# 1444-key attention: the full-array job of a key tile moves from in front of the tile's weighing to behind it

## The chip, the cores and the metric

The kernel runs on one core of a Trainium2 chip. The metric is the device time of one execution in microseconds (us), the median over several runs. Clocks and durations inside an execution come from one profiled execution.

## What is computed

Two decoder layers over 32 sequences of 100 tokens with 128 features. The part that matters here is the second layer's cross attention: 16 heads of 8 features attend from 100 tokens to 1444 context keys, for each of the 32 sequences.

```python
qm = split_heads(q @ Wq.T + bq);  km = split_heads(k @ Wk.T + bk);  vm = split_heads(v @ Wv.T + bv)
scores = einsum('bnlh,bnph->bnlp', qm, km) / sqrt(8)
scores = where(mask, scores, -1e8)
attn = softmax(scores, axis=-1)
out = einsum('bnlp,bnph->bnlh', attn, vm)      # then out @ Wo.T + bo
```

The softmax takes a maximum over the keys for each head and token, so scores are worked out twice: once for the maxima, once for the weights.

## The kernel before

The program has a setup and three stages. Stage A (self attention, first cross attention, gated feed-forward) and stage C (the last feed-forward with its experts) are not touched. Stage B (`stage_b`) is the attention above. It goes over 8 groups of 4 sequences: `n` is the sequence, `g` its group, `j` its place in the group.

For a sequence the keys are cut in 12 key tiles (`kt` 0 to 11) of 128 keys. TensorE's program, `slots`, goes through the key tiles and does three kinds of work in each:

- Scores. Four pieces (`score_piece`, p 0 to 3) work out the scores of the next key tile from 64 rows of the array each (L1304): pieces 0 and 1 on one half of the rows, 2 and 3 on the other. ScalarE takes the exponent of the results of two pieces at a time into `PT` (`exponent`, L1198).
- Ring jobs. Everything else that TensorE has to do for this or the next two sequences is cut into jobs (`job`), which write one PSUM bank each, of three banks in turn (`RING = (4, 5, 7)`). A job waits until the job three places ahead of it in the ring has been drained. Most jobs are maxima (L1285): one 64-row matmul with 482 keys, placed ahead of a score piece that uses the other half of the rows. VectorE drains each with a reduction (L1408).
- Weighing. `weigh` (L1320) multiplies `PT` of the tile with the values: 8 matmuls (16 instructions) in four column strips of 32, which all end in bank 6.

The rest of the ring jobs use all 128 rows; these are the full-array jobs. They stand at place `PHASES * kt + 4`, one place behind the last score piece of the tile:

| kt | maxima, on which pieces | full-array jobs | drained by |
|---|---|---|---|
| 0 | 4, on pieces 0 1 2 3 | queries of the next group: three for j = 0, one for j = 1 and 2, none for j = 3 | VectorE |
| 1 | 3, on 0 1 2 | the divisor of the sequence before ("result", L1267) | VectorE, one reciprocal (L1402) |
| 2 | 3, on 0 2 3 | value (L1272) | ScalarE copy (L1181) |
| 3 | 3, on 0 1 2 | value | ScalarE copy |
| 4 | 3, on 0 2 3 | value, the last of three | ScalarE, two copies |
| 5 | 3, on 0 1 2 | one query for j = 0 and 1 (L1256); leftover maximum (L1282) | VectorE |
| 6 | 3, on 0 2 3 | leftover maximum; key (L1261) | VectorE |
| 7 | 2, on 0 2 | leftover maximum; key | VectorE |
| 8 | none | turn of the maxima (L1289); key | VectorE (key: L1398) |
| 9, 10, 11 | 4, on 0 1 2 3 | none | |

A query job that is a "stack" (L1256) has three VectorE instructions behind it (L1382, L1385, L1386), of which the first frees the bank. VectorE drains strictly in ring order. The order of work is written out by hand (`MAIN_TILES`, `QUERY_SLOTS`, `ring_jobs`) and is fixed. The last sequences have fewer jobs: the last group has no queries, sequence 30 has no keys to prepare, and sequence 31 has only its result job.

`exponent` waits, ahead of its first half, for `pv_done` of the weighing two tiles back; `weigh` waits for the exponents of its own tile, for which the third score piece of the same tile has waited already.

Of the kernel before, what the change touches and what calls it, by code (L numbers as in the profile page):

```python
# [909 lines left out]
def ring_jobs(g, j, last):  # L910

    nxt = not last or j + 1 < GROUP
    after = not last or j + 2 < GROUP
    jobs = [((g, j + 1, "result", 0), PHASES * 1 + 4)]
    for i, (_, _, _, kt, p) in enumerate(MAINS):
        if i < EARLY and after:
            jobs.append(((g, j + 2, "max", i), PHASES * kt + p))
        if i >= EARLY and nxt:
            jobs.append(((g, j + 1, "max", i), PHASES * kt + p))
    if not last:  # L920
        jobs += [((g + 1, 0, "query", r), PHASES * kt + 4) for r, kt in QUERY_SLOTS[j]]
    if nxt:
        jobs += [((g, j + 1, "value", r), PHASES * (r + 2) + 4) for r in range(3)]
        jobs += [((g, j + 1, "max", len(MAINS) + c), PHASES * (c + 5) + 4) for c in range(3)]
        jobs.append(((g, j + 1, "turn", 0), PHASES * 8 + 4))
    if after:
        jobs += [((g, j + 2, "key", r), PHASES * (r + 6) + 4) for r in range(3)]
    return sorted(jobs, key=lambda job: job[1])
# [14 lines left out]
def stage_b(nc, t, ctxt, mask, pen_dram, h3t, att):  # L943
# [6 lines left out]
    with ExitStack() as ctx:  # L950
# [29 lines left out]
        def wait(engine, semaphore, value):  # L980

            if not (isinstance(value, int) and value <= 0):
                engine.wait_ge(semaphore, value)
# [16 lines left out]
        def place(g, j, i):  # L1000

            first = g if isinstance(g, int) else 1
            return starts[first, j] + i, (0 if isinstance(g, int) else g - 1)
# [230 lines left out]
        def _(pe):  # L1234
# [57 lines left out]
            def score_piece(g, j, kt, p):  # L1292

                n = g * GROUP + j
                half, a = divmod(p, 2)
                if kt == 0 and p == 0:
                    pe.wait_ge(t.ks_loaded[j % 2], (2 * g + (j // 2 + 1)) * 16 * KS_DMAS)
                    pe.wait_ge(t.qrow_loaded[j % 2], (2 * g + (j // 2 + 1)) * 64)
                    pe.wait_ge(sem["qexp_ready"], n + 1)
                if a == 0:  # L1300
                    wait(pe, sem["pt_ready"], n * 2 * KT + (2 * kt + half - 1))
                rows = slice(ROW * half, ROW * half + ROW)
                for s in (2 * a, 2 * a + 1):
                    m = mm(bank(p, D, 2 * T, (s % 2) * 2 * T), KS[rows, j % 2, s, kt * D:(kt + 1) * D],  # L1304
                           QS[rows, j % 2, s * 2 * T:(s + 1) * 2 * T], start=True, stop=True)
                if a:
                    m.then_inc(sem["st_psum"], 1)

            def weigh(g, j, kt):

                n = g * GROUP + j
                pe.wait_ge(sem["pt_ready"], n * 2 * KT + (2 * kt + 2))
                if kt == 0:
                    wait(pe, sem["att_free"], n)
                    pe.wait_ge(sem["v_drained"], 3 * (n + 1))


                for b in range(2):
                    for r in range(4):
                        m = mm(psum[32 * r:32 * r + 32, 6, b * 2 * T:(b + 1) * 2 * T], V[:, j % 2, kt, 4 * b + r, :],  # L1320
                               PT[:, kt % 2, 2 * b + r // 2, (r % 2) * 2 * T:(r % 2 + 1) * 2 * T],
                               start=(kt == 0 and b == 0), stop=(kt == KT - 1), tile_position=(0, 32 * r),
                               skip_group_check=True)
                m.then_inc(sem["pv_done"], 1)

            def slots(g, first, last):
                for j in range(GROUP):
                    jobs = ring_jobs(g, j, last)

                    def some(k):  # L1330
                        for i, (what, where) in enumerate(jobs):
                            if where == k:
                                job(*place(g, j, i), *what)

                    for kt in range(KT):

                        ahead = (j, kt + 1) if kt + 1 < KT else (j + 1, 0)
                        for p in range(4):
                            some(PHASES * kt + p)
                            if not last or ahead[0] < GROUP:  # L1340
                                score_piece(g, *ahead, p)
                        some(PHASES * kt + 4)
                        weigh(g, j, kt)

            for i, what in enumerate(first_ring_jobs()):
                job(i, 0, *what)
# [1 line left out]
            for p in range(4):  # L1348
                score_piece(0, 0, 0, p)
            slots(0, True, False)  # L1350
            for g in range(1, GROUPS - 1):
                slots(g, False, False)
            slots(GROUPS - 1, False, True)

            job(END, 0, GROUPS - 1, GROUP + 1, "result", 0)
# [888 lines left out]
```

## Time and profile before

| | |
|---|---|
| runs | 2407.42, 2407.45, 2408.70 us; median 2407.45 |
| profiled execution, its own time | 2401.97 us |
| its span, first to last instruction | 2400.2 us |
| maxima in stage B, first to last (L1285) | 643.0 to 1784.5 us |
| whole execution: PE, DVE, ACT, POOL busy | 85%, 66%, 55%, 22% |
| granted clock of TensorE, mean | 0.917 |

PE is TensorE's matmuls and PEld its weight loads, DVE is VectorE, ACT ScalarE, POOL GpSimd. The profiled execution is 0.23% below the median of the runs. A row of the timeline gives start, length, engine, line, operation, tiles, shapes and count; in brackets stands how long the engine was idle ahead of it and what ended that. Matmuls overlap, so PE can be shown as busy although it does not run at its full rate, and a row's length ends when its last result is out.

### The profile page before, as it was taken

The numbers are of one execution on the slowest core, as the hardware profiler recorded it, in microseconds if no ns is written. First come the engines' busy times: TensorE is split into PE (matmuls) and PEld (weight loads), VectorE is DVE, ScalarE is ACT, GpSimd is POOL, SyncE is SP. The second block draws the span as 40 slices with busy tenths as digits, with TensorE's granted clock in tenths as the row PEclk, the third lists the DMA queues.
The fourth block names the chain that finished last, engine by engine and source line by source line (L and its number), as shares of the span: only waits on it lengthen the run. The fifth ranks groups of instructions, "written<-read, shape, count | busy, mean of one in ns | idle before, by whom it ended". The sixth has DMA issues, their size and how long they took to land. (4 is left out here: it accounts for less than half of the span.)

```text
span 2400.2 us, 45166 instructions
## 1 busy us (share of the span) xinstructions
PE 2028.5 (85%) x17914; PEld 1347.5 (56%) x17914; DVE 1583.8 (66%) x3854; ACT 1320.0 (55%) x2169; POOL 535.9 (22%) x476
## 2 busy tenths in 40 slices
PE   3779997466599999999999999999996888878997
PEld 2546665343355556556565555556564565656776
DVE  5844543787578878877877878878862566654443
ACT  3645554576246666666666666666673555543333
POOL 1410000553302212212222212212212233221111
PEclk9789997666589999999999999999997898879999
DMA  5026662000222313313323323313312110000000
GB/s 160 1 86 187 186 186 75 4 18 17 90 69 104 115 64 113 114 64 117 107 77 108 107 72 113 115 62 115 115 43 94 35 36 18 1 1 4 8 8 11
DMA packets 89104, 181.18 MB, mean 75 GB/s; under 512 B 5907, under 2 KB 63163, under 8 KB 88511
## 3 DMA queue, kind: packets, MB, share of 16 engines
q1 hardware_dynamic: 88894, 178.30, 22.6%
q8 instruction: 143, 2.34, 0.4%
q14 instruction: 67, 0.54, 0.1%
HBM read 95.24 MB, written 11.65 MB: 45 GB/s over the span
## 5 line engine op out<-in xcount | busy, mean ns | idle before, releaser
L1408 DVE TENSOR_REDUCE b_part_max<-psum 128x1 f32<-128x482 f32 (+3 forms) x1248 | 737.3, 650 | 187.6 <-PE psum L1285 173.6
L1198 ACT ACTIVATE b_PT<-psum 128x800 f32<-128x800 f32 x768 | 616.4, 836 | 386.0 <-PE psum L1304 380.0
L1285 PE MATMUL psum<-b_KH,b_QBD 64*128 64x482 f32 (+1 forms) x1152 | 421.4, 443 | 46.3 <-DVE b_part_max L1408 43.4
L1304 PE MATMUL psum<-b_QS,b_KS 64*128 64x200 f32 x3072 | 438.7, 288 | 0.5 <-ACT b_PT L1198 0.3
L1304 PEld LDWEIGHTS psum<-b_QS,b_KS 64*128 64x128 f32 x3072 | 339.6, 186 | 16.2 <-issue 12.1
L1320 PE MATMUL psum<-b_PT,b_V 128*32 128x200 f32 x6144 | 341.1, 339 | 0.6 <-ACT b_PT L1198 0.6
L1285 PEld LDWEIGHTS psum<-b_KH,b_QBD 64*128 64x128 f32 x1152 | 196.6, 188 | 198.0 <-DVE b_part_max L1408 118.6
L1121 POOL TENSOR_TENSOR b_KL<-b_KF,b_KH 128x1444 fp32r<-128x1444 f32 x32 | 106.8, 3337 | 691.9 <-PE psum L1304 669.7
L1320 PEld LDWEIGHTS psum<-b_PT,b_V 128*32 128x32 f32 x6144 | 159.9, 109 | 149.0 <-ACT b_PT L1198 82.3
L2096 DVE SCALAR_TENSOR_TENSOR c_U<-psum,c_gt,c_U 100x128 f32<-100x128 f32 x256 | 72.1, 344 | 129.0 <-PE psum L1917 128.8
L384 POOL TENSOR_TENSOR a_rs<-a_ve,a_half 100x4 f32<-100x4 f32 x48 | 50.0, 1041 | 420.7 <-DVE a_ve L757 420.6
L1917 PE MATMUL psum<-c_W,c_HE 128*100 128x128 f32 x1024 | 123.6, 274 | 14.1 <-ACT c_HE L1682 14.0
L1917 PEld LDWEIGHTS psum<-c_W,c_HE 128*100 128x100 f32 x1024 | 117.2, 167 | 31.8 <-ACT c_HE L1682 18.7
L1272 PE MATMUL psum<-W,b_CT 128*128 128x128 f32 (+1 forms) x768 | 117.7, 293 | 12.7 <-DVE b_part_max L1408 6.7
L804 DVE TENSOR_REDUCE a_peak<-psum 100x1 f32<-100x1446 f32 x32 | 53.2, 1664 | 105.3 <-PE psum L629 105.3
L1272 PEld LDWEIGHTS psum<-W,b_CT 128*128 128x128 f32 (+1 forms) x768 | 92.7, 188 | 41.4 <-DVE b_part_max L1408 37.4
L1682 ACT ACTIVATE c_HE<-psum,C 128x400 f32<-128x400 f32 x128 | 71.9, 587 | 78.9 <-PE psum L1906 75.9
L1646 ACT COPY c_PT<-psum 100x800 f32<-100x800 f32 x64 | 52.5, 821 | 102.0 <-PE psum L1810 102.0
L636 PE MATMUL psum<-a_P,a_CN 128*128 128x100 f32 (+1 forms) x768 | 108.0, 288 | 0.0
L1261 PE MATMUL psum<-b_CT,W 128*128 128x482 f32 (+1 forms) x192 | 101.2, 611 | 5.5 <-DVE b_QF L1382 1.5
L636 PEld LDWEIGHTS psum<-a_P,a_CN 128*128 128x128 f32 (+1 forms) x768 | 95.2, 195 | 18.7 <-issue 11.8
L1535 POOL TENSOR_TENSOR c_rs<-c_ve,c_half 100x4 f32<-100x4 f32 x24 | 24.4, 1015 | 337.0 <-DVE c_ve L1998 337.0
(274 smaller groups left out, 3204.3 us busy)
## 6 DMA issues: line engine op xcount, KB each, us to landing
b_KS<-b_KH SPq DMA_DIRECT2D x64, 722.0 KB
a_CT<-in_ctxt SPq DMA_DIRECT2D x32, 722.0 KB, 4.2
b_CT<-in_ctxt SPq DMA_DIRECT2D x32, 722.0 KB, 4.3
b_KS<-b_KL SPq DMA_DIRECT2D x32, 722.0 KB
a_CN<-in_ctxn SPq DMA_DIRECT2D x32, 704.0 KB
att_scratch<-b_AO SPq DMA_DIRECT2D x32, 200.0 KB, 1.9
c_AIN<-att_scratch SPq DMA_DIRECT2D x8, 800.0 KB
b_MB<-in_mask SPq DMA_DIRECT2D x32, 180.5 KB, 4.4
```

The lines of the kernel that those rows point to most:

```text
L636: x_ = mm(bank(7, D, T, TG), CN[0:rows, m % 3, k, :], PTA[0:rows, m % 2, k, :], start=(k == 0), stop=(k == KT - 1))
L1121: pl.tensor_tensor(KL[:, :], KF[:, 0:S], KH[:, j % 2, :].bitcast(F32), ALU.subtract).then_inc(sem["kl_ready"], 1)
L1198: nc.scalar.activation(PT[:, kt % 2, 2 * a:2 * a + 2, :], psum[:, 2 * a:2 * a + 2, 0:TG], ACT.Exp).then_inc(sem["pt_ready"], 1)
L1261: m = mm(bank(b, D, size), w("xkT"), CT[:, j % 2, c:c + size], start=True, stop=True)
L1272: m = mm(bank(b, rows, D, (k % 4) * D), CT[:, j % 2, k * D:k * D + rows], w("xvT"), start=True, stop=True)
L1285: m = mm(bank(b, D, size), QBD[rows, j % 2, tile * D:(tile + 1) * D], KH[rows, j % 2, at_:at_ + size], start=True, stop=True)
L1304: m = mm(bank(p, D, 2 * T, (s % 2) * 2 * T), KS[rows, j % 2, s, kt * D:(kt + 1) * D], QS[rows, j % 2, s * 2 * T:(s + 1) * 2 * T], start=Tr ...
L1320: m = mm(psum[32 * r:32 * r + 32, 6, b * 2 * T:(b + 1) * 2 * T], V[:, j % 2, kt, 4 * b + r, :], PT[:, kt % 2, 2 * b + r // 2, (r % 2) * 2 ...
L1408: v.tensor_reduce(part_max[0:rows, q, c:c + 1], bank(b, rows, CHUNKS[c][1]), AX.X, ALU.max)\
L1682: nc.scalar.activation(HE[:, n % 2, f, :], bank((2 * n + f) % 4, D, TG), ACT.Relu, bias=t.C[:, c:c + 1]).then_inc(sem["moe_h_ready"], 1)
L1917: x_ = mm(bank(4 + n % 2, T, D, j * D), HE[:, n % 2, f, t.ts_(j)], W2[:, c * D:(c + 1) * D], start=(f == 0), stop=(f == 1))
L2096: last = v.scalar_tensor_tensor(out=U3[:, u % 2, j, :], in0=tok_bank(4 + n % 2)[:, j, :], scalar=gt[:, u, 6, j * EXPERTS + e:j * EXPERTS + ...
```

## The change

In each key tile the weighing is issued straight behind the last score piece, and the full-array jobs of the tile behind the weighing. No instruction is added or removed.

```diff
@@ -1339,8 +1339,8 @@
                             some(PHASES * kt + p)
                             if not last or ahead[0] < GROUP:
                                 score_piece(g, *ahead, p)
+                        weigh(g, j, kt)
                         some(PHASES * kt + 4)
-                        weigh(g, j, kt)
```

`some(k)` issues the ring jobs whose place is `k`. The other engines' programs are unchanged.

## Rows read from the trace of the kernel before

**Rows 1.** Windows, stage B at its steady rate: busy time, count, clock, DMA share, GB/s.
```profile
700.00:1760.00 1060.00, 984.03 (x10766) 622.86 (x10765) 852.27 (x1520) 678.30 (x946) 244.82 (x174) 1.00 0.28 96
```

**Rows 2.** The page's groups of instructions: the drain of maxima, weight load of values.
```profile
L1408 DVE TENSOR_REDUCE b_part_max<-psum 128x1 f32<-128x482 f32 (+3 forms) x1248 | 737.3, 650 | 187.6 <-PE psum L1285 173.6
...
L1272 PEld LDWEIGHTS psum<-W,b_CT 128*128 128x128 f32 (+1 forms) x768 | 92.7, 188 | 41.4 <-DVE b_part_max L1408 37.4
```

**Rows 3.** Timeline of PE, sequence 15, key tiles 1 and 2.
```profile
1231.20 0.48 PE L1285 MATMUL psum<-b_KH,b_QBD 64*128 64x482 f32 x1
...
1231.74 0.62 PE L1304 MATMUL psum<-b_QS,b_KS 64*128 64x200 f32 x4
1232.43 0.94 PE L1267 MATMUL psum<-b_OD,K 128*128 128x200 f32 x4
1233.30 0.89 PE L1320 MATMUL psum<-b_PT,b_V 128*32 128x200 f32 x16
1234.13 0.48 PE L1285 MATMUL psum<-b_KH,b_QBD 64*128 64x482 f32 x1
...
1234.90 0.46 PE L1285 MATMUL psum<-b_KH,b_QBD 64*128 64x482 f32 x1
...
1235.57 1.16 PE L1272 MATMUL psum<-W,b_CT 128*128 128x128 f32 x8 [0.22 <-DVE b_part_max L1408]
1236.66 0.89 PE L1320 MATMUL psum<-b_PT,b_V 128*32 128x200 f32 x16
```

**Rows 4.** Timeline of DVE in the same stretch.
```profile
1233.43 1.40 DVE L1402 RECIPROCAL b_RD<-psum 128x200 f32<-128x200 f32 x1
```

**Rows 5.** Timeline of ACT in the same stretch.
```profile
1236.77 0.59 ACT L1181 COPY b_V<-psum 128x512 f32<-128x512 f32 x1 [0.34 <-PE psum L1272]
```

**Rows 6.** Timeline of PE, the same sequence, weighings of key tiles 3 to 6.
```profile
1239.80 0.89 PE L1320 MATMUL psum<-b_PT,b_V 128*32 128x200 f32 x16
...
1243.05 0.89 PE L1320 MATMUL psum<-b_PT,b_V 128*32 128x200 f32 x16
...
1245.11 0.44 PE L1282 MATMUL psum<-b_KH,b_QBL 128*64 128x482 f32 x1
1245.48 0.88 PE L1320 MATMUL psum<-b_PT,b_V 128*32 128x200 f32 x16
...
1248.09 1.08 PE L1261 MATMUL psum<-b_CT,W 128*128 128x482 f32 x2
1249.09 0.89 PE L1320 MATMUL psum<-b_PT,b_V 128*32 128x200 f32 x16
```

**Rows 7.** Timeline of PE, sequence 13, key tiles 5 and 6, with a query.
```profile
1173.78 0.94 PE L1256 MATMUL psum<-b_HT,W 128*128 128x400 f32 x2
...
1174.87 0.88 PE L1320 MATMUL psum<-b_PT,b_V 128*32 128x200 f32 x16
...
1177.21 0.48 PE L1285 MATMUL psum<-b_KH,b_QBD 64*128 64x480 f32 x1 [0.59 <-DVE b_part_max L1408]
...
1179.35 0.89 PE L1320 MATMUL psum<-b_PT,b_V 128*32 128x200 f32 x16
```

**Rows 8.** Timeline of DVE in that stretch.
```profile
1174.78 0.62 DVE L1382 TENSOR_SCALAR b_QF<-psum,xbq 128x400 f32<-128x400 f32 x1
...
1176.51 2.91 DVE L1408 TENSOR_REDUCE b_part_max<-psum 64x1 f32<-64x482 f32 x5
```

**Rows 9.** Timeline of PE, sequence 15, key tile 9: first and fourth maximum.
```profile
1255.43 0.48 PE L1285 MATMUL psum<-b_KH,b_QBD 64*128 64x482 f32 x1
...
1256.67 0.48 PE L1285 MATMUL psum<-b_KH,b_QBD 64*128 64x482 f32 x1 [0.30 <-DVE b_part_max L1408]
```

**Rows 10.** Timeline of DVE there: the drain of the key job.
```profile
1254.72 0.72 DVE L1398 SCALAR_TENSOR_TENSOR b_KF<-psum,C,b_MB 128x480 f32<-128x480 f32 x1
```

**Rows 11.** Timeline of PE, sequence 16, key tile 0: fourth maximum, three queries.
```profile
1264.06 0.48 PE L1285 MATMUL psum<-b_KH,b_QBD 64*128 64x482 f32 x1 [0.29 <-DVE b_part_max L1408]
...
1264.63 1.62 PE L1253 MATMUL psum<-b_HT,W 128*128 128x136 f32 x6
```

## The prediction

> **What bounds the kernel now.** I read the page first, then stage B in windows, then who waits for whom on PE, then the timelines of PE, DVE and ACT over single key tiles. The window over the steady part of stage B shows PE busy for 984.03 of 1060.00 us at the full granted clock of 1.00 (2.4 GHz), DVE for 852.27 and ACT for 678.30 [rows 1]. So stage B goes at the pace of PE's instruction stream, and DVE, at 80%, is close behind. What PE does wait for is the ring: in each group of idle time the releaser is DVE's reduction of a maximum. The reader is to see in the timelines that the stage is regular to 0.02 us: the same key tile of another sequence with the same jobs takes the same time. So one sequence of each kind can be walked through and multiplied by its count.
>
> **What the change does.** It removes and adds nothing. It moves the full-array jobs of a key tile one weighing later. The weighing takes 0.82 us of PE (1233.30 to 1234.13, and 1174.87 to the next tile's start; I use 0.82) [rows 3, 7]. No DMA is issued by what is moved, and SP's and POOL's queues keep their order; their inputs (the turned maxima, the reciprocal) come up to 0.82 us later relative to the tile, and PE never waits for them now. Behind the moved jobs on PE now stand the next tile's scores and maxima directly.
>
> Two things follow, of opposite sign. First, a full-array job waits for the drain of the job three ahead of it, now just before it starts: the value job at 1235.57 shows 0.22 us idle for that [rows 3]. Behind a weighing this wait is over. Second, the job's own drain is what the third ring job behind it waits for, in the next tile a maximum. Before, that drain had the weighing and two pieces as cover; after, the pieces alone.
>
> **Prices that I use.** Changing between scores, weighing and full array, the next kind starts 0.06 to 0.07 us ahead of the modelled end of the last: result 1232.43+0.94=1233.37, weighing at 1233.30; weighing 1233.30+0.89=1234.19, maximum at 1234.13 [rows 3]. Slots, start to start: result 0.87, value 1.09 (1235.57 to 1236.66) [rows 3], leftover maximum 0.37, key 1.00 [rows 6], query stack with leftover maximum 1.09 (1173.78 to 1174.87) [rows 7]. The third value job needs 1.20: key tile 4 takes 3.25 (weighing to weighing, 1239.80 to 1243.05), less 1.23 for scores and wait and 0.82 [rows 6]. A bank is free for PE 0.05+0.65+0.06 us after the modelled end of a maximum (drain 650 ns [rows 2]; the fourth maximum at 1256.67 waits for the first, of 1255.43: 0.48+0.05+0.65+0.06=1.24) [rows 9]. Drains behind one another follow every 0.57 (five in 2.91) [rows 8]. From the last maximum to the next kind it is 0.41 where one piece follows (0.48−0.07) [rows 9] and 0.55 where two follow (0.62−0.07 from 1231.74) [rows 3]. So with maxima on 0 1 2 the third starts at 0.54 and scores end at 1.09; on 0 2 3 it starts at 0.77 and they end at 1.18 [rows 3].
>
> The one turn that no row shows is weighing to full array. I take it at 0.07 of overlap like the other three. The bounds: 0.05 us worse on each, or a first weight load of 0.19 us (188 ns [rows 2]) wholly under the weighing, so 0.12 to 0.19 better. The Trainium skill bears on this. "TensorE: Matmul & The Clock Gate", Part 2, step 1, says that TensorE pulls weight loads ahead of running matmuls where row groups don't collide or the background buffer takes them; that would give the better end. "TensorEngine Tiling", Key Properties, says that a change of tiling mode drains the engine; by that rule the trace agrees, since no turn above gains more than 0.07 us.
>
> **Tile by tile**, from the start of a tile's scores to that of the next, after minus before:
>
> - kt 0, three queries (7 sequences). The fourth maximum starts at 1.23. Before, the queries start 0.57 behind it (1264.06 to 1264.63) [rows 11]; scores alone end at 0.41, so 0.16 is wait. Between the three a further wait of about 0.24 shows (1.55 for their slots against 3×0.44, six matmuls with a step of some 0.22, an estimate from this row). After: −0.40, bounds −0.16 to −0.40; ×7 = −2.8.
> - kt 0, one query (14): −0.16; ×14 = −2.2.
> - kt 1, no single query ahead (18): 2.93 before (1231.20 to 1234.13) [rows 3]; after 1.09+0.82+0.87 = 2.78. −0.15; ×18 = −2.7. With one query ahead (14) its chain of three DVE instructions takes 1.73 (1174.78 to 1176.51) [rows 8] and now delays the third maximum by 0.27 and, through the first maximum's drain, the result job; this comes to 0.
> - kt 2 (31), the largest. Count from the start of kt 1's scores. Weighing at 1.09, result job at 1.91, its end at 2.85, reciprocal 0.06 later for 1.40 [rows 4]: 2.91 to 4.31, seen by PE at 4.37. The scores of kt 2 start at 2.78; their third maximum wants 3.55 and gets 4.37: 0.82 idle. Scores end at 4.78, weighing, value at 5.60 without a wait, next scores at 6.69. That is 3.91 against 3.36 (1233.30 to 1236.66) [rows 3]: +0.55; ×31 = +17.1.
> - kt 3 (31). The value job started at f=5.60; ends at f+1.16, copy at f+1.20 for 0.59 [rows 5], seen at f+1.85; scores started at f+1.09, so their third maximum goes at 0.76, not 0.54. 0.76+0.55+0.82+1.09 = 3.22 against 3.14 (1236.66 to 1239.80) [rows 3, 6]: +0.08; ×31 = +2.5.
> - kt 4 (31). Third maximum wants 0.77, no stall: 1.18+0.82+1.20 = 3.20 against 3.25 [rows 6]: −0.05; ×31 = −1.6.
> - kt 5 (31). As kt 3, third maximum at 0.76: 1.31+0.82+0.37 = 2.50 against 2.43 (1243.05 to 1245.48) [rows 6]; about +0.08 with a query as well; ×31 = +2.5.
> - kt 6, no query ahead (16). The leftover maximum's drain lets the third maximum go at 0.83: 1.24+0.82+0.37+1.00 = 3.43 against 3.61 (1245.48 to 1249.09), whose waits between scores, leftover and key go [rows 6]: −0.18; ×16 = −2.9.
> - kt 6, query ahead (14). Query at f, end f+0.94, DVE chain from f+1.00 for 1.73, leftover drain to f+3.38, seen at f+3.44 [rows 7, 8]. Scores start at f+1.09, so the third maximum goes at 2.35, where it went at 1.52 (1177.21 against 1175.69, which is 1174.87+0.82) [rows 7]. 2.35+0.41+0.82+0.37+1.00 = 4.95 against 4.48 (1174.87 to 1179.35) [rows 7]: +0.47; ×14 = +6.6.
> - kt 7, 8: 0, no third maximum and no wait of note.
> - kt 9 (30). The key job of kt 8 ends 0.07 behind the start of the scores; drain 0.12 to 0.84 [rows 10]; the third maximum goes at 0.90 (wanted 0.54). The first maximum's drain is queued behind it: 0.84 to 1.49, so the fourth goes at 1.55 where it went at 1.24 [rows 9]: +0.31; ×30 = +9.3. DVE has caught up by kt 10; 10 and 11: 0.
>
> Sum: +17.1+2.5+2.5+6.6+9.3 = +38.0 and −2.8−2.2−2.7−1.6−2.9 = −12.2: **+25.8 us**, all of it in stage B. The profiled execution would go from 2401.97 to 2427.8; on the median 2407.45, 0.23% above it, I predict **2433**. The same walk with the order of before gives the before rows to 0.02 us a tile, with nothing fitted but the slots. A change within 0.2%, or 5 us, is what a measurement of this kernel can't tell from none.
>
> **Rivals.**
>
> - A, cover only: the third maxima don't stall, as the banks come free in time. Then each tile keeps the gains: kt 0 and 1 −7.7; kt 2 (1.18+0.82+1.09=3.09) −0.27×31; kt 3 (3.00) −0.14×31; kt 4 −1.6; kt 5 (2.28) −0.15×31; kt 6 −0.23×16 and −0.35×14: −35, so 2372. Against it: the maximum at 1177.21 does stall, 0.59 of it shown, for just such a drain, with the weighing as cover still [rows 7]. Chance 0.04.
> - B, on the faster side: weighing to full array costs less than the other turns, with the first weight load under the weighing. 32 sequences have 8 such turns and three in four a ninth, some 270. At 0.19 each −51 against +26: 2382. It decides from 0.10 a turn (26/270). Against it: the three other turns hold at 0.06 to 0.07 [rows 3]. Chance 0.04; another 0.04 for a part of it that ends within 5 us of before. (The page on the clock gate, Part 2 of the Trainium skill, is the one that speaks for B.)
> - C, no change, 2407: DVE's and PE's waits only change places. That needs kt 2's reciprocal and kt 9's key drain off the ring's path, and both are on it by the ring rule. In the 0.04 above.
> - D, slower still: the stall in kt 6 behind a query, 1.58 long, brings PE's clock down to 1.2 GHz, where rows 1 show 1.00 throughout. If kt 7 then ran at half rate, some 2.5 us more for each of 14: 2468. Chance 0.04.
>
> **How the numbers follow.** Forecast 0.84. Its own range: ±0.05 on 270 turns is ±13, and the query estimate 2 more: 2419 to 2447. That range leaves out A, B and D, 0.12 in all, and a margin of the forecast's own; it is the range I give. Faster 0.08, same 0.04, slower 0.88.
>
> **What the profile after would show.** Third maximum of kt 2 idle for about 0.8 us behind the reciprocal, value and result jobs without idle ahead of them; period of kt 2 3.91, of kt 6 behind a query 4.95, of kt 9 2.78; a group of four sequences 3.3 us longer than now; clock 1.00 in stage B; stage A and C unchanged. Full-array jobs starting more than 0.07 before the end of a weighing would show B. What would make me wrong above all is that turn, and the reciprocal's drain overlapping otherwise than in the walk.

## The result and the profile after

The changed kernel takes 2428.34 us (median of 7 runs, 2425.01 to 2430.20) against 2407.45 (7 runs): ratio 1.0083, 95% interval 1.0069 to 1.0097. Slower, as forecast; 2433 was predicted, in a range of 2419 to 2447. The profiled execution took 2428.34 us with a span of 2426.6.

Stage B holds most of the difference. Its scores (L1304) run from 682.9 to 1814.1 us before and from 685.9 to 1836.0 after: 1131.2 against 1150.1, +18.9. The other 7.5 us between the two spans lie ahead of and behind the scores, where no code is changed. Over the ten profiled executions of this document the part ahead of the first score takes between 682.3 and 696.8 us and the part behind the last between 582.2 and 594.2, in no order that follows the edits, so this part of the difference is scatter.

The stage B window of the changed kernel; columns as in [rows 1]:

```profile
700.00:1780.00 1080.00, 1001.93 (x10796) 646.31 (x10796) 857.83 (x1521) 683.55 (x947) 245.14 (x174) 0.99 0.27 94
```

The clock is 0.99, not 1.00. What PE waited for in that window, longest in total first (us in total, times, longest):

```profile
PE psum L1285 <- DVE b_part_max L1408: 42.6, 101, 1.3
PE psum L1285 <- DVE b_RD L1402: 18.5, 29, 0.6
PE psum L1285 <- DVE b_KF L1398: 5.4, 30, 0.2
PE psum L1267 <- DVE b_part_max L1408: 3.6, 14, 0.3
```

Two new waits stand there, both of maxima (L1285): one for the reciprocal, once in each sequence, and one for the key's drain. The wait of the value job, which the same view of the kernel before (700 to 1760 us) shows, is gone from the list:

```profile
PE psum L1272 <- DVE b_part_max L1408: 6.3, 29, 0.2
```

Now the stretch of [rows 3], sequence 15, key tiles 1 and 2, after the change, on PE:

```profile
1245.44 0.48 PE L1285 MATMUL psum<-b_KH,b_QBD 64*128 64x482 f32 x1
...
1246.54 0.89 PE L1320 MATMUL psum<-b_PT,b_V 128*32 128x200 f32 x16
1247.36 0.94 PE L1267 MATMUL psum<-b_OD,K 128*128 128x200 f32 x4
1248.23 0.48 PE L1285 MATMUL psum<-b_KH,b_QBD 64*128 64x482 f32 x1
...
1249.80 0.48 PE L1285 MATMUL psum<-b_KH,b_QBD 64*128 64x482 f32 x1 [0.64 <-DVE b_RD L1402]
...
1250.21 0.88 PE L1320 MATMUL psum<-b_PT,b_V 128*32 128x200 f32 x16
1251.02 1.16 PE L1272 MATMUL psum<-W,b_CT 128*128 128x128 f32 x8
1252.11 0.48 PE L1285 MATMUL psum<-b_KH,b_QBD 64*128 64x482 f32 x1
```

and on DVE, the answer to [rows 4]:

```profile
1248.34 1.41 DVE L1402 RECIPROCAL b_RD<-psum 128x200 f32<-128x200 f32 x1 [0.58 <-PE psum L1267]
```

The reader is to see four things. The weighing ends, as modelled, at 1246.54+0.89=1247.43, and the result job starts at 1247.36: the turn that no row had shown overlaps by 0.07 us like the others. The third maximum of key tile 2 starts 1.57 us into the tile (1249.80 against 1248.23), 0.8 later than it could; the prediction's walk through the tile had 1.59. The value job starts with no idle ahead of it. And the tile takes 1252.11−1248.23=3.88, where 3.91 was forecast and 3.36 measured before.

The profile gives each tile of each sequence. Measured change of the tiles' lengths, summed over sequences 0 to 30, beside the prediction's terms:

| key tile | before, us | after, us | sum measured | sum forecast |
|---|---|---|---|---|
| 0, three queries / one | 4.18 / 3.49 | 3.42 / 3.33 | −6.9 | −5.0 |
| 1 | 2.93 (3.45 behind one query) | 2.79 to 2.84 (3.44) | −2.1 | −2.7 |
| 2 | 3.36 | 3.89 | +16.4 | +17.1 |
| 3 | 3.14 | 3.28 | +4.2 | +2.5 |
| 4 | 3.25 | 3.18 | −2.4 | −1.6 |
| 5, with query / without | 3.13 / 2.41 | 3.32 / 2.60 | +5.7 | +2.5 |
| 6, behind query / not | 4.48 / 3.62 | 4.74 at full clock / 3.21 | +2.8, with the half clock told below | +3.7 |
| 7 | 3.06 | 2.85 | −5.3 | 0 |
| 9 | 2.47 | 2.68 | +6.4 | +9.3 |
| 8, 10, 11 | 2.47 | 2.47 | 0 | 0 |
| all | | | +18.8 | +25.8 |

Two rows fall out of the walk. Key tile 7 became shorter, and in four sequences (0, 8, 12 and 20, all with j = 0) key tiles 6 and 7 together take 1.57 us more than elsewhere. For the second, sequence 12 (PE, the stretch that answers to [rows 7]):

```profile
1149.76 0.48 PE L1285 MATMUL psum<-b_KH,b_QBD 64*128 64x480 f32 x1
...
1152.10 0.48 PE L1285 MATMUL psum<-b_KH,b_QBD 64*128 64x480 f32 x1 [1.28 <-DVE b_part_max L1408]
...
1152.51 1.56 PE L1320 MATMUL psum<-b_PT,b_V 128*32 128x200 f32 x16
1154.00 0.66 PE L1282 MATMUL psum<-b_KH,b_QBL 128*64 128x482 f32 x1
1154.46 1.69 PE L1261 MATMUL psum<-b_CT,W 128*128 128x482 f32 x2
1156.08 0.49 PE L1285 MATMUL psum<-b_KH,b_QBD 64*128 64x480 f32 x1
```

The third maximum goes 2.34 us into the tile, as forecast (2.35): 1.57 later than the 0.77 at which it could, and 1.28 of that is shown as idle. Behind it everything is slow: the weighing takes 1.56 us and not 0.89. Three windows of PE alone (busy time and count, then the granted clock), and the stall and what follows it in sequence 13, where the same stall has no such sequel:

```profile
1149.00:1152.00 3.00, 1.82 (x11) 1.00 0.00 0
1152.60:1155.60 3.00, 3.00 (x19) 0.50 0.00 0
1156.20:1159.20 3.00, 3.00 (x33) 1.00 0.02 5
1189.00:1191.60 2.60, 1.50 (x10) 1.00 0.00 0
1191.80:1195.00 3.20, 3.20 (x32) 1.00 0.00 0
```

TensorE is at 0.50, that is 1.2 GHz, right behind the stall in sequence 12, and at 1.00 in sequence 13. This is rival D, which had a chance of 0.04 and put 2.5 us on each of 14 places. It came in 4 of them, in this one execution, at 1.57 us each, 6.3 us in all.

For key tile 7, weight loads (PEld) of its leftover maximum and key job. After, sequence 12:

```profile
1157.76 0.13 PEld L1282 LDWEIGHTS psum<-b_KH,b_QBL 128*64 128x64 f32 x1 [0.32 <-DVE b_part_max L1408]
1157.81 0.41 PEld L1261 LDWEIGHTS psum<-b_CT,W 128*128 128x128 f32 x2
1158.93 0.42 PEld L1304 LDWEIGHTS psum<-b_QS,b_KS 64*128 64x128 f32 x6 [0.71 <-ACT b_PT L1198]
```

Before, sequence 15:

```profile
1250.76 0.13 PEld L1282 LDWEIGHTS psum<-b_KH,b_QBL 128*64 128x64 f32 x1
1251.13 0.30 PEld L1261 LDWEIGHTS psum<-b_CT,W 128*128 128x128 f32 x2 [0.24 <-DVE b_part_max L1408]
1252.14 0.33 PEld L1320 LDWEIGHTS psum<-b_PT,b_V 128*32 128x32 f32 x12 [0.71 <-ACT b_PT L1198]
```

Before, the key's first weight load waits for a bank and starts 0.37 us behind that of the leftover maximum. After, the bank is free by then and the load starts 0.05 us behind it, under the running matmul. The matmuls of the same two jobs, after and before:

```profile
1157.76 0.43 PE L1282 MATMUL psum<-b_KH,b_QBL 128*64 128x480 f32 x1
1158.03 0.97 PE L1261 MATMUL psum<-b_CT,W 128*128 128x482 f32 x2
...
1250.76 0.44 PE L1282 MATMUL psum<-b_KH,b_QBL 128*64 128x480 f32 x1
1251.13 1.08 PE L1261 MATMUL psum<-b_CT,W 128*128 128x482 f32 x2
```

Leftover and key take 1158.93−1157.76=1.17 us together and not 1252.14−1250.76=1.38. Half of the gain is an earlier start of the key (0.27 us behind the leftover and not 0.37), half a shorter key (0.90 to the next kind and not 1.01).

### The profile page after: what moved, and what is told of

Its sections match the earlier page's. It is cut to its first block and busy times, and to the rows that moved or that the text cites. A ratio compares the mean times of both kernels' runs of the same rounds, so it can differ in the third digit from the quotient of the medians.

```text
span 2426.6 us, 45166 instructions
## 1 busy us (share of the span) xinstructions
PE 2055.2 (85%) x17914; PEld 1376.2 (57%) x17914; DVE 1591.2 (66%) x3854; ACT 1324.3 (55%) x2169; POOL 536.6 (22%) x476
## 3 DMA queue, kind: packets, MB, share of 16 engines
q8 instruction: 143, 2.34, 0.4%
## 5 line engine op out<-in xcount | busy, mean ns | idle before, releaser
L1285 PE MATMUL psum<-b_KH,b_QBD 64*128 64x482 f32 (+1 forms) x1152 | 460.8, 457 | 80.2 <-DVE b_part_max L1408 44.0
L1304 PE MATMUL psum<-b_QS,b_KS 64*128 64x200 f32 x3072 | 483.9, 294 | 0.6 <-ACT b_PT L1198 0.3
L1304 PEld LDWEIGHTS psum<-b_QS,b_KS 64*128 64x128 f32 x3072 | 360.0, 187 | 27.8 <-ACT b_PT L1198 25.4
L1285 PEld LDWEIGHTS psum<-b_KH,b_QBD 64*128 64x128 f32 x1152 | 200.3, 188 | 272.4 <-DVE b_part_max L1408 152.6
L1906 PE MATMUL psum<-c_YT,c_W 128*128 128x400 f32 x256 | 98.1, 506 | 0.0
```

Source lines behind the costliest of these rows:

```text
L1285: m = mm(bank(b, D, size), QBD[rows, j % 2, tile * D:(tile + 1) * D], KH[rows, j % 2, at_:at_ + size], start=True, stop=True)
L1906: mm(bank((2 * n + f) % 4, D, TG), W1[:, c * D:(c + 1) * D], YT[:, u, :], start=True, stop=True).then_inc(sem["moe_h_psum"], 1)
```

## The experiments

Ratios are against the kernel before, whose median beside these kernels was 2410.02 for the first four and 2410.07 for the last four. Two theories stood against each other. One is late drains: the prediction's walk, with the slots of key and queries corrected by the profile above. The other is an even cost of the turn from weighing to full array, which the total of 20 us on 270 turns does not exclude.

Times of whole executions scatter by some us, mostly outside stage B, so for each kernel the length of stage B in its profiled execution is given too, from its first score to its last (L1304):

| kernel | stage B, us | against before | against changed |
|---|---|---|---|
| before | 1131.2 | | |
| changed | 1150.1 | +18.9 | |
| result job alone behind | 1144.4 | +13.2 | |
| result job alone in front | 1138.2 | | −11.9 |
| query tile in front | 1132.5 | | −17.6 |
| key tiles 6 and 7 alone | 1108.5 | −22.7 | |
| copy, order of before | 1124.8 | −6.4 | |
| copy, changed order | 1122.1 | | −28.0 |
| long chain | 1177.0 | | +26.9 |
| only the jobs that gain | 1098.7 | −32.5 | |

### One job moved: the result job alone behind the weighing

```diff
-                        weigh(g, j, kt)
-                        some(PHASES * kt + 4)
+                        if kt != 1:
+                            some(PHASES * kt + 4)
+                            weigh(g, j, kt)
+                        else:
+                            weigh(g, j, kt)
+                            some(PHASES * kt + 4)
```

> The order of before, with the result job of key tile 1 alone behind its weighing. Theory (late drains: what costs is that the job's drain now comes too late for the third ring job behind it): key tile 1 falls from 2.93 to 2.78 us (3.50-less case 3.44 to 2.78 behind a query), key tile 2 rises from 3.36 to about 4.19, as its third maximum stalls 0.8 behind the reciprocal and the value job then waits too; about +14 us, 2421. Rival (the cost is spread evenly: each of some 270 turns from weighing to full array costs about 0.075 us, which makes the 20 us of the change): 31 turns, +2 us, 2410, and key tile 2 stays at 3.36.

Measured: 2427.34 us, ratio 1.0068 (1.0044 to 1.0093), +16. Sequence 15 on PE, its key tile 2:

```profile
1247.50 0.49 PE L1285 MATMUL psum<-b_KH,b_QBD 64*128 64x482 f32 x1
...
1249.07 0.48 PE L1285 MATMUL psum<-b_KH,b_QBD 64*128 64x482 f32 x1 [0.64 <-DVE b_RD L1406]
...
1249.77 1.16 PE L1272 MATMUL psum<-W,b_CT 128*128 128x128 f32 x8 [0.21 <-DVE b_part_max L1412]
1250.86 0.89 PE L1320 MATMUL psum<-b_PT,b_V 128*32 128x200 f32 x16
1251.68 0.48 PE L1285 MATMUL psum<-b_KH,b_QBD 64*128 64x482 f32 x1
```

Key tile 2 takes 1251.68−1247.50=4.18 us (forecast 4.19); key tile 1 fell to 2.75 to 2.79. The third maximum stalls behind the reciprocal, and as the value job is still in front it waits too. An even cost of a turn would give +2 us. This one moved job of some nine costs by itself 13.2 us of stage B, where the whole change costs 18.9.

### The mirror: the result job alone in front

The condition is `kt == 1` for the order of before, all else as changed.

> The changed order, with the result job of key tile 1 alone back in front of its weighing. Late drains: key tile 2 falls from 3.89 to 3.09 us (no stall behind the reciprocal, and no wait ahead of the value job), key tile 1 is 2.93, but 4.26 behind a single query (its result waits in front for a drain queue that the query has delayed); together -12 us against the changed kernel, about 2416. Even cost of a turn: -2 us, 2426.

Measured: 2414.07 us, ratio 1.0024 (1.0010 to 1.0039). Key tile 2 takes 3.08, key tile 1 2.93 and, behind one query, 4.26. So taking the same job out of the changed kernel gives most of the loss back. Four half-clock stretches are there again, two of them in key tile 6 behind the query and two in key tile 1 behind one query, where the result job now waits 1.1 us. One of the latter, sequence 17:

```profile
1318.12 1.25 PE L1267 MATMUL psum<-b_OD,K 128*128 128x200 f32 x4 [1.07 <-DVE b_part_max L1412]
1319.29 1.56 PE L1320 MATMUL psum<-b_PT,b_V 128*32 128x200 f32 x16
```

### The query tile in front

The condition is `kt == 5 and j < 2`.

> The changed order, with the jobs of key tile 5 back in front of the weighing for the two sequences of a group that have a query there. Late drains: key tile 6 behind the query falls from 4.74 to 3.93 us, its third maximum stalling 0.75 and not 1.57; -12 us, and, if the four stretches of half clock seen in the changed kernel come from the long stall, these go too and give some 5 us more: about 2411. Even cost of a turn: 14 turns fewer, -1 us, 2427; and half clock would be seen as before.

Measured: 2410.14 us, ratio 1.0001 (0.9987 to 1.0015). The stretch of [rows 7] on PE:

```profile
1179.39 0.48 PE L1285 MATMUL psum<-b_KH,b_QBD 64*128 64x480 f32 x1
...
1180.91 0.48 PE L1285 MATMUL psum<-b_KH,b_QBD 64*128 64x480 f32 x1 [0.59 <-DVE b_part_max L1412]
...
1183.30 0.48 PE L1285 MATMUL psum<-b_KH,b_QBD 64*128 64x480 f32 x1
```

The third maximum goes at 1.52 as before the change, key tile 6 takes 3.91 (forecast 3.93), and the clock is 1.00 from 700 to 1760 us. The other jobs stay moved, and the kernel is level with the kernel before. Of the 17.6 us of stage B that this gives back, 14 times 0.82 are the tile and 6.3 the half clock.

### The key tiles 6 and 7 alone

The condition is `kt not in (6, 7)`.

> The order of before, with the jobs of key tiles 6 and 7 (leftover maximum and key) alone behind the weighing. Late drains: nothing queued behind them is late enough to stall, and the gains stand alone. Their waits go, and the key's weight load, no longer held by a wait, slides under the leftover maximum: key tile 6 falls from 4.48 to 3.93 us behind a query and from 3.62 to 3.17 without, key tile 7 from 3.05 to 2.86; about -22 us against before, 2386. Even cost of a turn: 60 turns, +4 us, 2412.

Measured: 2385.59 us, ratio 0.9911 (0.9893 to 0.9929). Key tile 6 takes 3.93 behind a query and 3.07 else (forecast 3.17), key tile 7 2.85. Sequence 15, its key tile 7 on PE, without a wait:

```profile
1238.54 0.48 PE L1285 MATMUL psum<-b_KH,b_QBD 64*128 64x480 f32 x1
...
1240.21 0.43 PE L1282 MATMUL psum<-b_KH,b_QBL 128*64 128x480 f32 x1
1240.48 0.97 PE L1261 MATMUL psum<-b_CT,W 128*128 128x482 f32 x2
1241.38 0.70 PE L1304 MATMUL psum<-b_QS,b_KS 64*128 64x200 f32 x8
```

So two of the moved places are worth 23 us of stage B by themselves, and the same edit that makes the kernel slower as a whole makes it faster there.

### The reciprocal made short, in either order

```diff
-                    v.reciprocal(RD[:, :], bank(b, D, PAIRED // 2)).then_inc(drained, 1)
+                    v.tensor_copy(RD[:, :], bank(b, D, PAIRED // 2)).then_inc(drained, 1)
```

The copy leaves out the reciprocal, so the output is not the attention's; the kernels serve to time the order alone. In the order of before:

> The order of before, with the reciprocal of the divisor (1.40 us on VectorE) replaced by a copy of the same 128x200 elements, so that the output is not the attention's; a copy should take some 0.4 us. Late drains: the drain is hidden in this order but for the value job's wait; key tile 2 falls from 3.36 to 3.15 us, -7 us against before, 2403. If the reciprocal played no part in key tile 2: nothing.

and in the changed order:

> The changed order with the same copy in place of the reciprocal. Late drains: the third maximum of key tile 2 no longer stalls, and key tile 2 falls from 3.89 to 3.09 us: -25 us against the changed kernel, 2403, level with the same copy in the order of before (-5 us by the walk, the half-clock stretches taking that back). Even cost of a turn: the copy changes both orders alike, and this one stays 20 us above the other, 2423.

Measured: 2403.27 us, ratio 0.9973 (0.9957 to 0.9990), and 2398.56 us, ratio 0.9954 (0.9939 to 0.9969). The changed order with the copy, on DVE and then on PE:

```profile
1229.72 0.37 DVE L1402 COPY b_RD<-psum 128x200 f32<-128x200 f32 x1 [0.58 <-PE psum L1267]
```

```profile
1229.61 0.48 PE L1285 MATMUL psum<-b_KH,b_QBD 64*128 64x482 f32 x1
1229.62 0.88 PE L1304 MATMUL psum<-b_QS,b_KS 64*128 64x200 f32 x7
...
1230.39 0.37 PE L1285 MATMUL psum<-b_KH,b_QBD 64*128 64x482 f32 x1
...
1232.60 0.48 PE L1285 MATMUL psum<-b_KH,b_QBD 64*128 64x482 f32 x1
```

With a drain of 0.37 us and not 1.41 the third maximum goes at 0.78, without a stall, and key tile 2 takes 2.99. In the order of before it takes 3.14. The order of before gets 7 us from the shorter drain and the changed order some 30 (28 in stage B, where 25 were expected, the tile being 0.1 shorter than expected), and the changed order is then no longer the slower one. Four half-clock stretches stand behind the 14 long stalls of key tile 6 here too. What the change costs in key tile 2 hangs on the length of this one drain.

### The long chain made longer

In the changed order the third instruction of a query stack is issued twice:

```diff
+                    link(v.scalar_tensor_tensor(out=QR[:, g % 2, s, :], in0=QH[:, :].bitcast(F32), scalar=K[:, K_NEG1:K_NEG1 + 1],
+                                                in1=QF[:, :], op0=ALU.mult, op1=ALU.add))
                     m = v.scalar_tensor_tensor(out=QR[:, g % 2, s, :], in0=QH[:, :].bitcast(F32), scalar=K[:, K_NEG1:K_NEG1 + 1],
                                                in1=QF[:, :], op0=ALU.mult, op1=ALU.add)
```

> The changed order, with the third VectorE instruction of each query stack issued twice in a row, 0.64 us longer (the result is the same). Late drains: key tile 6 behind a query rises from 4.74 to 5.40 us, its stall from 1.57 to 2.2, and key tile 1 behind one query from 3.44 to 4.10; 28 times 0.66 is +18 us against the changed kernel, 2447. If the long stall is what brings half clock, there are more than the four stretches of the changed kernel, up to one behind each of the 14 stalls, and 2450 to 2465; if these stretches have another cause, about four again.

Measured: 2456.87 us, ratio 1.0196 (1.0178 to 1.0215), 0.0113 or 27 us above the changed kernel's 1.0083; 28 times 0.66 and five half-clock stretches more at 1.57 make 26, and stage B grew by 26.9. Key tile 1 behind one query takes 4.11 (forecast 4.10); key tile 6 behind the query takes 5.42 at full clock and 6.96 where half clock follows. Sequence 13 on PE:

```profile
1213.21 0.48 PE L1285 MATMUL psum<-b_KH,b_QBD 64*128 64x480 f32 x1
...
1216.22 0.70 PE L1285 MATMUL psum<-b_KH,b_QBD 64*128 64x480 f32 x1 [1.95 <-DVE b_part_max L1410]
...
1216.85 1.56 PE L1320 MATMUL psum<-b_PT,b_V 128*32 128x200 f32 x16
```

Half clock now follows in 9 of 14 such tiles, and seven of the nine are those at j = 1, one in every group. So the stalls of one execution are no independent draws, and each count here is that of one execution. A stall of 1.28 us of shown idle was followed by half clock in 4, 4 and 2 of 14 places (the changed kernel, the changed order with the copy, the result job in front), one of 1.95 in 9 of 14, and in the six kernels whose longest idle in stage B's steady part is 0.65 us there is none. Taking the stall away took the half clock away, and making it longer brought more. So the stall brings it. Why one stall of the same length is followed by it and the next is not, none of these runs shows.

### Only the jobs that gain

The order of before, with the jobs of key tiles 3, 6 and 7 behind the weighing, and those of key tile 0 for j = 0 (`if not (kt in (3, 6, 7) or kt == 0 and j == 0)` keeps the old order).

> Behind the weighing stand only the jobs that the walk says gain there: those of key tiles 3, 6 and 7, and of key tile 0 for the sequence with three queries. Late drains: key tile 0 with three queries 3.42 us, key tile 3 3.00, key tile 6 3.93 behind a query and 3.07 without, key tile 7 2.85, the rest as before, no half clock; -31 us against before, 2379. Even cost of a turn: some 100 turns, +7 us.

Measured: 2380.73 us, ratio 0.9876 (0.9857 to 0.9895), −30. Key tile 0 with three queries takes 3.42, key tile 3 2.97, key tile 6 3.93 and 3.07, key tile 7 2.85, the others as before. It beats both kernels. Stage B is 32.5 us shorter than before, where 31 was expected. In the window at its steady rate the clock is 1.00:

```profile
700.00:1730.00 1030.00, 967.96 (x10801) 631.22 (x10800) 855.76 (x1520) 678.99 (x946) 244.79 (x174) 1.00 0.29 99
```

PE issues 10801 matmuls in 1030 us, where 10766 took 1060 [rows 1].

## Why the prediction was right

- What bounds the kernel: right. Stage B goes at PE's stream, and the idle time in it belongs to the ring. With the slots corrected by the profile after, the tile lengths named in the expectations of eight further kernels came out within 0.10 us, most within 0.03.
- First effect, the wait in front of a full-array job goes: right. The value job starts without a wait, and where the gains stand alone they are worth 23 us of stage B (key tiles 6 and 7) and 33 (all the jobs that gain).
- Second effect, the job's drain loses the weighing as cover: right, and the larger of the two in the changed kernel. It was shown from both sides, by moving the result job alone and by taking it back alone, and by shortening the drain.
- The turn from weighing to full array: 0.07 us of overlap, as taken (1247.43 against 1247.36), so rival B is out. For comparison, the key job behind the leftover maximum, with both on all 128 rows, starts 0.16 us ahead of the end (1157.76+0.43=1158.19 against 1158.03). The Trainium skill, "TensorEngine Tiling (Array Packing)", Key Properties, has a change of tiling mode drain the engine; the trace agrees in so far as this turn overlaps less than that one.
- Key tiles 6 and 7: mis-sized. The terms of key tile 6 and "kt 7, 8: 0" took 1.00 us for a key job, from a row in which it had waited for its bank. For key tile 7 "no wait of note" was wrong too: the key's weight load waits 0.24 us there. Without the wait leftover and key take 1.17 and not 1.37: 0.20 in each of some 60 tiles, 12 us, nearly all that the sum was too high. The Trainium skill, "TensorE: Matmul & The Clock Gate", Part 2, step 1, has weight loads pulled ahead of running matmuls. The trace agrees here: as soon as no wait holds it, the key's load starts 0.05 us behind the leftover's, while the leftover maximum runs.
- Smaller terms: three queries in a row gain 0.76, where the bounds were 0.16 to 0.40, as behind the weighing they take 0.95 us together and not 3×0.44; a stalled third maximum with two pieces behind it needs 0.62 to the end of the scores and not 0.55 (key tiles 3 and 5: +9.9 and not +5.0); in key tile 9 the first maximum's drain starts 0.63 behind the key's and not 0.72 (+6.4 and not +9.3). They cancel to about 1 us.
- Half clock, put at 0.04 as rival D with 35 us, came in part: four stretches, 6.3 us. Summed: 25.8−13.3+6.3=18.8 us in stage B. The walk was 13.3 us too high, and the half clock made up 6.3 of it. Of the 7 us that were left in stage B the medians show 5 (20.9 between them, 25.6 forecast), and the 2 us between are scatter outside it. Without the half clock the change would have been some 12.5 us in stage B, which on the median of before is 2420, at the lower end of the range. That part of the closeness is luck.

## What to carry to other kernels

In a ring of buffers a job has two times that matter: the wait in front of it, and the moment by which its drain must be over for the job one ring length behind. Moving it later helps the first and hurts the second, so it has to be priced for each job by the length of its drain, and the answer can differ in sign between neighbours: here two places of one edit gained 23 us of stage B and a third lost 13. A slot that was read from a row with a wait in it is too long for an order in which the wait is gone, and a stall that is made longer may cost more than its own length through the clock.

## What the runs showed of the hardware

A stall of PE shown as 1.28 us idle, between stretches at full clock, was followed by half clock in 4, 4 and 2 of 14 places in three kernels, one of 1.07 us in 2 of 14, and one of 1.95 us in 9 of 14; each time it cost 1.4 to 1.6 us beside the wait. Waits of 0.65 us had none behind them, nor had the 14 of 0.9 us in key tile 1 of the long chain. A weight load that waits for a bank loses its place under the matmul ahead of it: the pair of leftover maximum and key took 1.38 us with a wait of 0.24 ahead of the key's load and 1.17 without it. A change between 64-row pieces, column strips and full array overlapped by 0.06 to 0.07 us in every direction seen, and the key job behind the leftover maximum, both on all 128 rows, by 0.16.
